# Cross attention of layer 1: TensorE sums two tiles of a head in place of six, DMA nine, GpSimd sixteen

## What is computed

```python
q = (query @ Wq.T).reshape(B, 512, 16, 32).transpose(0, 2, 1, 3)
k = (key @ Wk.T).reshape(B, 8192, 16, 32).transpose(0, 2, 1, 3)
v = (value @ Wv.T).reshape(B, 8192, 16, 32).transpose(0, 2, 1, 3)
attn = softmax(einsum('bhqd,bhkd->bhqk', q, k) * 32 ** -0.5)
x = einsum('bhqk,bhkd->bhqd', attn, v)          # all heads side by side
return x @ Wo.T + bo
```

## Time and profile before

| | |
|---|---|
| median of three runs | 4505.09 us |
| the profiled execution | 4505.94 us |
| its span, first to last instruction | 4503.9 us |
| TensorE busy | 3998.8 us, 89% |
| VectorE busy | 3010.0 us, 67% |
| ScalarE busy | 2216.3 us, 49% |
| GpSimd busy | 1667.3 us, 37% |
| mean granted TensorE clock | 0.931 |

### The profile page before, as it was taken

How to read it: one execution, slowest core, us unless ns; L and a number is a source line. 1 busy time by engine, 2 the same in 40 slices (tenths; PEclk the granted TensorE clock), 3 DMA queues, 4 the chain that set the end, 5 groups by cost and what they waited for, 6 DMA issues and landing times. The chain is left out here.

```text
span 4503.9 us, 51238 instructions
## 1 busy us (share of the span) xinstructions
PE 3998.8 (89%) x17936; PEld 2238.5 (50%) x17936; DVE 3010.0 (67%) x3608; ACT 2216.3 (49%) x3355; POOL 1667.3 (37%) x984
## 2 busy tenths in 40 slices
PE   7995899999999686678999779999999988769997
PEld 6883444444444251137777534444444325447775
DVE  3333877777786259945777657777878634467776
ACT  2221466565656333313766416666666631336764
POOL 0001487778778506500000026666666630000000
PEclk9997899999999778979999869999999988789998
DMA  8998566666666300021888636666666540318886
GB/s 308 326 335 274 145 149 149 148 150 148 147 149 145 102 14 0 0 85 64 306 300 303 243 114 153 153 151 152 145 149 146 125 103 9 96 46 309 301 302 229
DMA packets 301551, 751.70 MB, mean 167 GB/s; under 512 B 55793, under 2 KB 89330, under 8 KB 268017
## 3 DMA queue, kind: packets, MB, share of 16 engines
q1 hardware_dynamic: 245136, 560.20, 36.9%
q0 software_dynamic: 47456, 171.46, 18.8%
q10 hardware_dynamic: 8704, 16.78, 1.1%
HBM read 484.23 MB, written 98.37 MB: 129 GB/s over the span
## 5 line engine op out<-in xcount | busy, mean ns | idle before, releaser
L746 ACT ACTIVATE prob<-psum 128x512 f32<-128x512 f32 x1552 | 894.1, 597 | 543.3 <-PE psum L644 498.6
L644 PE MATMUL psum<-q_stack,k_ring 98*128 98x512 f32 x2048 | 1025.2, 519 | 20.0 <-ACT prob L746 14.6
L914 POOL TENSOR_TENSOR den_pool<-den_pool,prob 128x1024 f32<-128x1024 f32 x372 | 935.8, 2516 | 224.0 <-DVE den_pool L826 155.2
L621 PE MATMUL psum<-k_ring,q_stack 96*128 96x512 f32 x2048 | 690.4, 421 | 104.7 <-DMA k_ring<-k_lo 35.6
L797 DVE CUSTOM_DVE_ANT_0 psum<-psum,mask_q 128x1024 f32<-128x1024 f32 x512 | 627.9, 1232 | 222.9 <-PE psum L621 205.4
L793 DVE TENSOR_REDUCE row_max<-psum 128x1 f32<-128x1024 f32 x512 | 614.6, 1219 | 230.8 <-PE psum L621 228.1
L1881 DVE TENSOR_TENSOR weight_lo<-weight_raw,weight_hi 128x2048 fp32r<-128x2048 f32 x240 | 546.9, 2289 | 162.7 <-ACT weight_hi L1824 162.5
L644 PEld LDWEIGHTS psum<-q_stack,k_ring 98*128 98x128 f32 x2048 | 397.9, 195 | 403.1 <-ACT prob L746 275.4
L662 PE MATMUL psum<-prob,x 128*32 128x512 f32 x3104 | 514.7, 608 | 0.9 <-ACT prob L746 0.9
L621 PEld LDWEIGHTS psum<-k_ring,q_stack 96*128 96x128 f32 x2048 | 394.8, 200 | 215.3 <-issue 79.1
L1824 ACT ACTIVATE weight_hi<-weight_raw 128x2048 fp32r<-128x2048 f32 x240 | 453.9, 1915 | 41.7 <-DMA weight_raw<-in_L_ffn_w 22.8
(11 more groups left out here) (421 smaller groups left out, 6362.0 us busy)
## 6 DMA issues: line engine op xcount, KB each, us to landing
weight_raw<-in_L_ffn_w SPq DMA_DIRECT2D x120, 1024.0 KB, 6.4
den_dma<-prob POOLq DMA_DIRECT2D x204, 512.0 KB, 4.9
k_ring<-k_hi SPq DMA_DIRECT2D x1024, 64.0 KB, 2.1
weight_raw<-in_L_ffn_Wu SPq DMA_DIRECT2D x60, 1024.0 KB, 7.1
weight_raw<-in_L_ffn_Wd SPq DMA_DIRECT2D x60, 1024.0 KB, 5.0
den_dma<-xnT POOLq DMA_DIRECT2D x68, 512.0 KB, 4.9
k_ring<-k_lo SPq DMA_DIRECT2D x512, 64.0 KB, 2.4
ctxT<-in_ctxT SPq DMA_DIRECT2D x16, 1024.0 KB, 9.0
```

The costliest lines, as they stand in the source:

```text
L621: ins = e.matmul(max_banks(q)[:, a * KC:(a + 1) * KC], q_stack[h % n_q][0:QROWS, i * P:(i + 1) * P], k_ring[0:QROWS, (n + a) % kring, :], ...
L644: e.matmul(k.bank(b % 2), k_ring[:, n % kring, kt * P:(kt + 1) * P], q_stack[h % n_q][:], start=not masked, stop=True).then_inc(s_score, 1)
L746: e.activation(prob[b // 2 % n_p][:, b % 2, :], k.bank(b % 2), ACT.Exp, scale=scale).then_inc(s_exp, 1)
L914: e.tensor_tensor(den[:], den[:], tile, ALU.add).then_inc(s_dpool, 1)
```

## The change

In layer 1 TensorE sums the tiles of pairs 21 and 27 instead of those of 12, 15, 18, 21, 24 and 27. The DMA takes nine pairs, 5, 8, 11 and so on up to 29, instead of eight (7, 10, 13, 16, 19, 22, 25, 29). GpSimd has what is left: 6, 7, 9, 10, 12, 13, 15, 16, 18, 19, 22, 24, 25, 28, 30 and 31, which are 16 pairs instead of 13 (5, 6, 8, 9, 11, 14, 17, 20, 23, 26, 28, 30, 31). VectorE keeps its five pairs. `Waves` follows from it: 4 sums instead of 12, so 17 waves a head instead of 19. Waves run in pairs 2, 4, 6, 8, 10, 12, 14, 16, 18, 20, 22, 24, 25, 27, 29, 30 and in pair 0 of the next head; before in 2, 4, 6, 8, 10, 12, 14, 15, 17, 18, 20, 21, 23, 24, 26, 27, 29, 30 and 0. The masked branch, layer 0's, is as it was: VectorE five pairs, DMA nine, GpSimd 18, TensorE none.

```diff
     if masked:
         sums = Sums([0, 1, 2, 3, 4], [], list(range(5, PAIRS - 2, 3)))
     else:
-        sums = Sums([0, 1, 2, 3, 4], [12, 15, 18, 21, 24, 27], [7, 10, 13, 16, 19, 22, 25, 29])
+        sums = Sums([0, 1, 2, 3, 4], [21, 27], list(range(5, PAIRS - 2, 3)))
     waves = Waves(sums.by_pe)
```

## The result

| | before | after |
|---|---|---|
| median of seven runs each, side by side | 4507.87 us | 4519.01 us |
| lowest to highest | 4501.05 to 4510.14 | 4513.44 to 4522.94 |
| the profiled execution | 4505.94 us | 4516.85 us |
| its span | 4503.9 us | 4514.9 us |
| TensorE busy | 3998.8 us | 3991.8 us |

The ratio is 1.0027, with a 95% interval of [1.0017, 1.0037]: slower by 0.27%, some 12 us. Forecast were 4489 us, and a range of 4475 to 4504 that doesn't hold the result.

What follows compares the result with a forecast made beforehand. It took TensorE as full (765 of 794.7 us) in layer 1's cross attention, with a wave costing 0.94 us where ScalarE limits. Terms -28.2 + 3 + 3 + 5.3 + 1 = -15.9 gave 4489 us, range 4475 to 4504.

Steps and rivals of the forecast that it cites:

- The wave (1): TensorE in layer 1's cross attention: two waves fewer a head at 0.94 us each, -28.2 us over 15 heads.
- GpSimd's round (2): GpSimd's 16 adds and nine DMA adds a head: about 50 us from first add to merge, costing nothing directly.
- The collision (3): VectorE's first add of a head sometimes waits for GpSimd's last add: +3 us over 14 heads.
- rival three: Slower: in every head VectorE's first add waits for GpSimd's last and the clock dips; 4535 us, chance 0.08.
- Layer 0 as evidence against: Argument against the slower outcome: layer 0, 18 adds a head under a longer period, has first adds of 1.22 us throughout.
- Heads 4, 8 and 12 (4): VectorE limits pairs 16 to 23 there, so one of two dropped waves buys nothing: +3 us.
- The end (5): Head 15, end of the stage: GpSimd's adds start later and its last merge lands later, with nothing to hide it: +5.3 us.
- The clock (6): TensorE's clock drops to its lower level after a wait in pair 8; one more such dip: +1 us.
- rival two: GpSimd's loop sets the pace and a head gains only 0.3 to 1 us: about 4503 us, chance 0.20.

Runs made afterwards that it cites:

- e1: Changed kernel's TensorE part alone, 17 waves; GpSimd and DMA keep their earlier pairs, and pairs 12, 15, 18, 24 are summed by nobody: 4500.5 us.
- e8: Changed kernel with the reciprocals and divides of heads 4, 8 and 12 moved to every second pair from 12 to 26: 4501.2 us.
- e2: Changed kernel with GpSimd leaving out its last two adds of each head, pairs 30 and 31: 4491.4 us.
- e4: Changed kernel with two den_dma tiles, one for even and one for odd heads, so a head's first DMA needn't wait for the previous merge: 4510.3 us.
- e7: Changed kernel with one more TensorE matmul per pair in head 15, its result never read: 4520.4 us.
- e9: Changed kernel with DMA adds going to two sums in turn and the reciprocals and divides spread over pairs 12 to 26: 4470.4 us.
- e11: Changed kernel with two DMA sums, divides spread, VectorE making GpSimd's adds in head 15, no TensorE sums, eleven DMA adds: 4453.7 us.
- e5: Changed kernel with its DMA adds going to two tiles in turn, each with its own merge: 4496.9 us.

## Why the prediction was wrong, step by step

**The wave (1) was right**: 1.92 us a head measured for two waves, 1.88 forecast, and a wave is worth nearly the same three times over (quiet heads of 60.14 us with 19 waves, 59.2 with 18, 58.2 with 17, 57.24 with 16).

**GpSimd's round (2) is the step that failed.** I built it up from stretches of the trace, "I call it 50", for 16 adds, and didn't make the same sum for the kernel before. The rows ahead of the prediction give that one: first add 13.1 behind the mark, merge 5.3 behind the next, a period of 60.17, so 52.4 us with 13 adds. The profile's mean over all heads was 51.6. A round that gets three adds and a DMA add more and yet is 2.4 us shorter should have stopped me. What was undersized is the chain. Means over heads 0 to 14 of after, beside the terms of the prediction: the two adds ahead of the second DMA 4.9 (4.9); the five stretches of issue and two adds 30.2 (28.6); the two of issue and one add 11.3 (10.2); the last issue to the merge 6.9 (6.05). With three pairs in 4.98 us (one and a half times the 3.32 of the earlier trace rows) DMA adds are asked for as fast as they land, so a landing over its median holds up the queue and one under it gives nothing back, and each needs about 0.5 us more until the next is issued. I had taken the median for the mean of such a chain, and left that half microsecond out. The round was 53.3, not 50.

**The collision (3)**, forecast at 3 us, cost 21.6 (pairs 6 to 10, 23.7 less 2.1, with the clock's share): nine heads of 14 at 2.6 us each. The mechanism and the place were those of rival three, down to the divide between hit and not hit: it gave "ends over 4.8 behind the mark in every head", and the measured bound of 7.8 behind the first exponential, with the mark 2.6 behind that and the merge 0.3 behind the last add, is 4.9. I gave it 0.08 and too small a spread: "a cover of 0.3 and a spread of 1", where the rounds spread over 5 us. Its "in every head" was too much, nine of 14, and so was its 4535: of the five heads that were not hit, four follow a head that its own losses had made 5 to 8 us longer (4, 7, 8, 12), and so gave GpSimd's round that much more room. Not foreseen at all was that the second adds are hit too, that VectorE's add gets in between GpSimd's two and delays the later, and that no extra GpSimd work is needed (e1). The rule of the Trainium skill (SBUF — State Buffer, Who interferes with whom), that the port pair which the two share is "an exclusive lock", holds in every one of these rows: the later add waits out the earlier one, while VectorE's reduction between its two adds, whose input is in PSUM, took its usual 1.21 us.

**Layer 0 as evidence against** was worth nothing: its first adds of 1.22 say that 18 adds fit into its period, and I never worked out how much room that leaves.

**Heads 4, 8 and 12 (4)** cost 6.3 us instead of 3 (16.7 less 10.4). Two or three of the divides are hit in each, as foreseen as a possibility and left out of the term. e8 shows the whole of it to hang on divides in consecutive pairs.

**The end (5)**, forecast at 5.3, cost 9.9. Head 14's merge came 13.0 us into head 15, not 8.1 (5.5 behind the mark), since the DMA add of pair 29 took 8.9 us to land, the longest of the stage; so the adds start at 18.7, not at 14.0. Beside it ran the load of the output weights, 1024 KB, which SyncE issues 2.0 us into head 15. SyncE's and GpSimd's timelines of after:
```profile
3587.17 0.53 SPq L600 DMA_DIRECT2D w_out<-in_L_xattn_WoT  x1
```
```profile
3588.72 0.88 POOL L896 DMA_DIRECT2D den_dma<-prob  x1 [1.74 <-DMA den_dma<-prob]
```
Before, pair 29's add went out 2.3 us ahead of the load and landed in 4.8. In all five profiles in which it goes out 1.5 to 2 us behind the load (after, e2, e4, e7, e8) it takes 7.9 to 8.9 us, 7.0 where it goes out 0.4 ahead of it (e1), and 4.4 to 5.1 where it goes out more than 2 us ahead. No run moved the load, so the cause is argued from these times. A late GpSimd round thus cost more here than its lateness, which the step had no term for. From there on the step was right: a round of 49.6 (50), and 4.6 to land. GpSimd's last merge and TensorE's wait for it in after, as in the earlier trace rows:
```profile
3653.44 0.88 POOL L890 DMA_DIRECT2D den_pool<-den_dma  x1 [0.30 <-POOL den_pool L914]
```
```profile
3658.15 1.03 PE L674 MATMUL psum<-o_sb,comb 128*32 128x512 f32 x1 [3.52 <-DMA den_pool<-den_dma]
```

**The clock (6)**, forecast at 1 us, is for the most part inside the 21.6 of (3): in heads 1 to 14 the clock was at half for 27.2 us more, 23.9 of them from pair 8 on, behind the collisions, and 3.4 in pairs 22 to 24 of heads 4, 8 and 12. How much of the 21.6 is the clock's and how much VectorE's was not measured apart.

Together: -26.9 + 21.6 + 6.3 + 9.9, with head 0's 2.1 the other way, is +8.8, and the stage went from 1001.4 to 1010.1 us; the rest of the profiled difference of 10.9 is in stages that the change doesn't touch. The range failed with (2): its upper end came from rival two, which lets GpSimd eat the gain and stops there.

## What to carry to other kernels

When a change shortens the period of a loop, work out for every engine that ends its round in the next period how much room it had and has, and make the sum for the known kernel first; a sum that doesn't give today's number can't give tomorrow's. A chain of DMAs that each wait for the last is as long as its landings, whatever the DMA's share of busy time; two chains in turn cost a tile and a merge, and took the round here from 53 us to 46 to 48. And where a shared resource makes an engine wait a whole instruction, a move of a few tenths of a microsecond decides between nothing and 2 to 3 us: then put slack between the two instead of counting on the mean.

## What the runs showed of the hardware that I had not expected

- A VectorE add that waits for GpSimd goes ahead between two GpSimd adds that stand back to back: the last two adds of a head took 6.0 to 6.3 us where VectorE's add got in between, and 4.9 to 5.2 where it didn't (after), and both engines lose.
- DMA adds of 512 KB within SBUF land in 5.1 us in the median with the DMA engines at 0.64 (before), 5.0 at 0.67 (after), 5.3 at 0.75 (e9) and 5.6 at 0.84 (e11); e9 and e11 also have two of them under way at a time, so the share and the pairing aren't told apart. The five that took 8.8 to 9.6 us (the last of head 14 in after, e2 and e4, the last of head 15 in e5 and e9) all run beside a transfer of 1024 KB from SyncE's queue.
- After a wait of 1.26 us in head 15 the granted clock was at half for 30.7 us (e1); in the heads with maxima a dip behind a wait for VectorE lasts 3.4 to 10.2 us. In head 15 the same code was at half for 13.7 us in one execution (after) and not at all in another (e8), with a matmul more per pair not at all either (e7).
